# Score stacks of 64 rows in the two row halves of the TensorE array, and the steps of the first attention in pairs

## The reference

```python
# layer 0: keys are the context's 361 and the 100 own rows
qkv = _layernorm(x) @ w_attn + b_attn
q, k, v = jnp.split(qkv, 3, axis=2)
kc, vc = jnp.split(ctx @ w_ref + b_ref, 2, axis=2)
key, value = concat([kc, k]), concat([vc, v])
w = einsum('bhtd,bhsd->bhts', qh, kh) / sqrt(16)    # masks, and -2 on the context's columns
a = einsum('bhts,bhsd->bhtd', softmax(w), vh)
x = x + tanh(g_xattn[0]) * (a @ w_proj + b_proj)
x = x + tanh(g_ffn[0]) * quantised_ffn(_layernorm(x))          # 704 wide, rounded to 8 bits
# layer 1: queries from x, keys and values from the context alone
scores = einsum('bhqd,bhkd->bhqk', query, key) / sqrt(16)
x = x + tanh(g_xattn[1]) * (einsum('bhqk,bhkd->bhqd', softmax(scores), value) @ w_o.T + b_o)
x = x + tanh(g_ffn[1]) * top2_of_8_experts(_layernorm(x))      # 1024 wide
```

## Time and profile before

| | us |
|---|---|
| three runs, median (lowest, highest) | 663.76 (663.71, 664.19) |
| the profiled execution, its span | 664.1 |
| PE busy in it | 515.1 (78%) |
| PEld busy | 356.1 (54%) |
| DVE busy | 429.5 (65%) |
| ACT busy | 297.8 (45%) |
| POOL busy | 162.6 (24%) |
| mean granted TensorE clock | 0.861 of full |
| the eight rounds of the first attention | 24.7, 24.6, 25.7, 23.1, 23.0, 23.0, 24.1; the last 19.6 |
| the eight rounds of the second attention | 13.6, 18.5, 17.2, 13.3, 14.1, 13.4, 14.5; the last 11.2 |

### The profile page before, as it was taken

How to read it: one execution, slowest core, us unless ns; L and a number is a source line. 1 busy time by engine, 2 the same in 40 slices (tenths; PEclk the granted TensorE clock), 3 DMA queues, 4 the chain that set the end, 5 groups by cost and what they waited for, 6 DMA issues and landing times. The chain is left out here.

```text
span 664.1 us, 15475 instructions
## 1 busy us (share of the span) xinstructions
PE 515.1 (78%) x5403; PEld 356.1 (54%) x5403; DVE 429.5 (65%) x921; ACT 297.8 (45%) x482; POOL 162.6 (24%) x191
## 2 busy tenths in 40 slices
PE   2477798998988898737547878998975269999994
PEld 1263365665666667523223545655654258887782
DVE  7365576667686774387754856777569875666662
ACT  6442145556556538203314546676753223333331
POOL 5500022122122211010045410122125044444432
PEclk9989588979999977668659788999976569999997
DMA  9136834444535700000073787789347111222210
GB/s 258 40 120 113 161 82 105 105 115 110 112 99 140 188 5 25 1 1 0 0 154 88 181 155 151 142 165 178 121 158 270 60 40 28 48 40 47 49 19 1
DMA packets 73247, 64.31 MB, mean 97 GB/s; under 512 B 33326, under 2 KB 65750, under 8 KB 73190
## 3 DMA queue, kind: packets, MB, share of 16 engines
q1 hardware_dynamic: 61544, 41.37, 28.3%
q0 software_dynamic: 8224, 21.06, 12.0%
q10 hardware_dynamic: 3424, 1.12, 0.8%
HBM read 48.59 MB, written 15.92 MB: 97 GB/s over the span
## 5 line engine op out<-in xcount | busy, mean ns | idle before, releaser
L467 PEld LDWEIGHTS PS<-QS,KS 112*120 112x120 f16 (+2 forms) x896 | 81.9, 144 | 29.9 <-issue 10.9
L467 PE MATMUL PS<-QS,KS 112*120 112x100 f16 (+2 forms) x896 | 92.8, 229 | 5.1 <-ACT PT L530 3.7
L578 DVE CUSTOM_DVE_ANT_0 PS<-PS,maskv 100x461 f32<-100x461 f32 x128 | 80.5, 647 | 15.2 <-PE PS L436 14.3
L581 DVE TENSOR_REDUCE mx<-PS 100x1 f32<-100x361 f32 x128 | 63.6, 529 | 35.8 <-PE PS L439 34.7
L530 ACT ACTIVATE PT<-PS 120x400 f32<-120x400 f32 (+1 forms) x128 | 63.4, 503 | 45.5 <-PE PS L467 43.1
L530 ACT ACTIVATE PT<-PS,ctxb 120x400 f32<-120x400 f32 (+1 forms) x96 | 57.0, 596 | 52.7 <-PE PS L467 51.9
L436 PE MATMUL PS<-KS,QS 65*100 65x461 f16 x128 | 52.6, 416 | 17.9 <-DVE mx L578 17.3
L795 POOL TENSOR_SCALAR_AFFINE_SELECT PT<-PT 100x400 f32<-100x400 f32 x32 | 17.7, 553 | 187.6 <-ACT PT L530 187.6
L2025 PE MATMUL PS<-aT,WE 128*128 128x128 f16 x960 | 59.4, 224 | 0.0
L2025 PEld LDWEIGHTS PS<-aT,WE 128*128 x960 | 57.0, 101 | 0.0
L2038 PE MATMUL PS<-WE,hidden_high 128*128 x160 | 53.0, 379 | 0.0
(11 more groups left out here) (307 smaller groups left out, 1069.7 us busy)
## 6 DMA issues: line engine op xcount, KB each, us to landing
share<-in_L_ffn_w_dram POOLq DMA_DIRECT2D x13, 1024.0 KB, 9.3
k_scratch<-share SPq DMA_DIRECT2D x32, 180.5 KB, 2.5
KS<-k_scratch SPq DMA_DIRECT2D x32, 180.5 KB, 3.6
KS<-k_scratch SPq DMA_DIRECT2D x64, 90.2 KB, 6.3
QS<-q_scratch SPq DMA_DIRECT2D x64, 50.0 KB, 2.7
v_scratch<-xn SPq DMA_DIRECT2D x8, 385.7 KB
values_staged<-v_scratch SPq DMA_DIRECT2D x8, 385.7 KB
WE<-in_L_ffn_w_dram POOLq DMA_DIRECT2D x2, 1024.0 KB, 8.6
```

What stands on the lines that cost most here:

```text
L467: last = nc.tensor.matmul(bank[0:kn, i * T:(i + 1) * T], KS[p][:, h, k0:k0 + kn], QS[p][:, h, :], start=True, stop=True)
L578: nc.vector.tensor_tensor_reduce(rows, rows, maskv[:, :], 1.0, -BIG, ALU.add, ALU.max, mx[p][:, h:h + 1]).then_inc(s_smf, 1)
L581: nc.vector.tensor_reduce(mx[p][:, h:h + 1], sm_bank[h % 2][0:T, 0:TC], X, ALU.max).then_inc(s_smf, 1)
```

## The change

Of the four products of halves the one of the two low halves is left out of the scores. A head's stack now has 64 rows: 0 to 31 the query's high half against both key halves, 32 to 47 the delta and maximum rows, 48 to 63 the query's low half against the key's high half. The stacks of even batches lie at partitions 0 to 63, those of odd ones at 64 to 127, so that SM of batch o+1 and ST of batch o use different row halves of the array. SM reads all 64 rows; the rows of the maxima are zero at that time, which a third, zero plane of the queries' DRAM copy provides with each load. Per half of the heads a stack takes 7 loads (QS 3, own keys 2, context keys 2), of key bytes 3 parts instead of 4. In the second attention it is 3 for QS, and 2 for a group's keys, of 32 and 16 rows.

In setup ACT's two copies and the clearing of zero rows go; one POOL copy spreads `delta` over both key stacks at once (128 partitions x 7376), DVE clears QS (128 x 1600), two DMAs write the zero plane.

Steps of the first attention go in pairs: PE runs SM, ST, SM, ST of two steps, and then the T, K, V groups and the PV that the two steps had; ACT does both exponentials before the copies, DVE both maxima before the differences. In the second attention SM goes ahead of ST (a second SM behind it), and the unread matmul and PV follow.

```diff
-    KROWS = 4 * DH
-    IROW = 96
-    KX = IROW + H
+    KX = 4 * DH
+    IROW = 2 * DH
...
-        KSa = in_all("KS", [P, 2, H, S0], F16)
-        KS = [KSa[0:KX, p] for p in range(2)]
-        QS = [in_all(f"QS{p}", [KX, H, T], F16) for p in range(2)]
+        KSa = in_all("KS", [P, H, S0], F16)
+        QSa = in_all("QS", [P, H, T], F16)
+        KS, QS = ([a[p * KX:(p + 1) * KX] for p in range(2)] for a in (KSa, QSa))
...
         def pe_SM(pe, j, o, h, layer, smn):
-                nc.tensor.matmul(bank[0:T, 0:S0], QS[p][0:KROWS + 1, h, :], KS[p][0:KROWS + 1, h, :],
-                                 start=True, stop=True).then_inc(s_smd, 1)
...
+            n = S0 if layer == 0 else TC
+            nc.tensor.matmul(bank[0:T, 0:n], QS[p][:, h, :], KS[p][:, h, 0:n], start=True, stop=True
+                             ).then_inc(s_smd, 1)
...
         def act_max_rows(act, j, o, part, nmc):
-            nc.scalar.activation(QS[p][IROW:KX, hs, :], misc[NB][0:H, 0:T].unsqueeze(1).to_broadcast([H, n, T]),
+            nc.scalar.activation(QS[p][IROW:IROW + H, hs, :], misc[NB][0:H, 0:T].unsqueeze(1).to_broadcast([H, n, T]),
...
         def sp_queries_in(sp, j, o, mb):
-                sp.dma_start(QS[o % 2][s_:KROWS:2, hs, :], src).then_inc(s_ks[o % 2][mb], 16)
+                sp.dma_start(QS[o % 2][s_:IROW:2, hs, :], q_dram[hs, 0, :, ts].rearrange("h d t -> d h t")
+                             ).then_inc(s_ks[o % 2][mb], 16)
+            sp.dma_start(QS[o % 2][IROW:KX, hs, :], q_dram[hs, 1:3, :, ts].rearrange("h a d t -> (a d) h t")
+                         ).then_inc(s_ks[o % 2][mb], 16)
         def sp_keys_in(sp, j, o, hs, dst, dram, own, done):
-            for a in range(2):
-                sp.dma_start(dst[a * 2 * DH:(a + 1) * 2 * DH, hs, :], src).then_inc(done, 16)
+            sp.dma_start(dst[0:IROW, hs, :], src.rearrange("h d s t -> (d s) h t")).then_inc(done, 16)
+            sp.dma_start(dst[IROW + H:KX, hs, :], src[:, :, 0, :].rearrange("h d t -> d h t")).then_inc(done, 16)
...
@@ SP, setup
+                sp.wait_ge(s_kz, 1)
+                for mb in range(KC):
+                    sp.dma_start(q_dram[mb * HM:(mb + 1) * HM, 1, :, :],
+                                 QSa[:, 0:HM, :].rearrange("p h t -> p (h t)")).then_inc(s_qw, 16)
...
+                sp.wait_ge(s_kr, 1)
                 sp.wait_ge(s_kw[0][0], KW)
                 for mb in range(KC):
                     sp_stack0(sp, 0, 0, mb)
...
@@ POOL, setup
-                nc.gpsimd.memset(KS[0][KROWS:IROW, HM:H, :], 0.0)
-                nc.gpsimd.memset(KS[1][KROWS:IROW, 0:HM, :], 0.0)
-                nc.gpsimd.memset(KS[1][KROWS:IROW, HM:H, :], 0.0).then_inc(s_kz, 1)
+                nc.gpsimd.tensor_copy(KSa[:, :, :], delta[:, :].unsqueeze(2).to_broadcast([P, H, S0])).then_inc(s_kr, 1)
...
@@ ACT, setup
-                act.wait_ge(s_dl, 1)
-                for p in range(2):
-                    nc.scalar.activation(KS[p][IROW:KX, :, :], delta[:, :].unsqueeze(2).to_broadcast([H, H, S0]), ACT.Copy
-                                         ).then_inc(s_kr, 1)
                 act.wait_ge(s_wr[0], 16)
                 nc.scalar.activation(wah[:, :, :], r_attn, ACT.Copy, scale=WS).then_inc(s_wh8, 1)
...
@@ PE, rounds of the first attention
-                    for t in range(16):
-                        if t == 4:
-                            pe.wait_ge(s_vsb[u], j + 1)
-                        pe_ST(pe, j, u, t, 0, 0, 0)
-                        if t == NTURN0 and not first:
+                    for t in range(0, 16, 2):
+                        for i in (t, t + 1):
+                            if nxt:
+                                pe_SM(pe, j, u + 1, i, 0, 0)
+                            if i == 4:
+                                pe.wait_ge(s_vsb[u], j + 1)
+                            pe_ST(pe, j, u, i, 0, 0, 0)
+                        if t == NTURN0 - 1 and not first:
                             pe_turn(pe, j, u - 1, 0)
...
@@ PE, rounds of the second attention
                     for t in range(NST1):
+                        sms = SMH1[t] if nxt else 0
+                        if sms > 0:
+                            pe_SM(pe, j, o + 1, h, 1, SMN)
+                            h += 1
                         pe_ST(pe, j, o, t, 1, STN, 2 * B)
+                        if sms > 1:
+                            pe_SM(pe, j, o + 1, h, 1, SMN)
+                            h += 1
                         unread()
...
-                            for _ in range(SMH1[t]):
-                                pe_SM(pe, j, o + 1, h, 1, SMN)
-                                h += 1
```

More of the change, by code:

```diff
@@ L881, in round0 @@
                     nh0 = MISC0 + MISCR * (2 * j + u)
-                    for t in range(16):
-                        act_exp(act, j, u, t, 0, 0)
-                        if t == 0 and not first:
-                            act_max_rows(act, j, u, 1, 0)
-                        if t == 1 and not first:
-                            act_evac(act, j, u - 1, 0)
-                        if weights and 1 <= t < 1 + NIB + KC:
-                            rounding(NIB + t - 1)
-                        kind = TVK.get(t, "")
-                        if keys and kind[:1] == "T":
-                            act_hi_T(act, j, u + 2, int(kind[1]), nh0 + int(kind[1]))
-                        elif keys and kind[:1] == "K":
-                            act_hi_K(act, j, u + 2, int(kind[1]), nh0 + NK0[int(kind[1])])
+                    for t in range(0, 16, 2):
+                        for i in (t, t + 1):
+                            act_exp(act, j, u, i, 0, 0)
+                            if i == 0 and not first:
+                                act_max_rows(act, j, u, 1, 0)
+                        for i in (t, t + 1):
+                            if i == 1 and not first:
+                                act_evac(act, j, u - 1, 0)
+                            if weights and 1 <= i < 1 + NIB + KC:
+                                rounding(NIB + i - 1)
+                            kind = TVK.get(i, "")
+                            if keys and kind[:1] == "T":
+                                act_hi_T(act, j, u + 2, int(kind[1]), nh0 + int(kind[1]))
+                            elif keys and kind[:1] == "K":
+                                act_hi_K(act, j, u + 2, int(kind[1]), nh0 + NK0[int(kind[1])])
                     if nxt:
@@ L1013, in _ @@
             def _(dve):
-                for p in range(2):
-                    nc.vector.memset(QS[p][KROWS:IROW, :, :], 0.0)
-                nc.vector.memset(KS[0][KROWS:IROW, 0:HM, :], 0.0)
+                nc.vector.memset(QSa[:, :, :], 0.0).then_inc(s_kz, 1)
                 dve.wait_ge(s_x, 32)
@@ L1099, in round0 @@
                     nv = n0 + (NV0 if keys else 0)
-                    for t in range(16):
-                        if t == NTURN0 and not first:
-                            dve_norm(dve, j, u - 1, 0)
-                        if first and t == 8:
-                            dve_bias_in(dve, 0)
-                        if weights and t in WMT:
-                            weight_maxima(WMT.index(t))
-                        kind = TVK.get(t, "")
-                        if keys and kind[:1] == "T":
-                            dve_lo_T(dve, j, u + 2, int(kind[1]), n0 + int(kind[1]), nh0 + int(kind[1]))
-                        elif keys and kind[:1] == "K":
-                            k = int(kind[1])
-                            dve_lo_K(dve, j, u + 2, k, n0 + NK0[k], nh0 + 2 + k)
-                        elif nxt and kind[:1] == "V":
-                            dve_V(dve, j, u + 1, int(kind[1]), nv + int(kind[1]))
-                        if nxt:
-                            dve_max(dve, j, u + 1, t, 0, 0)
+                    for t in range(0, 16, 2):
+                        for i in (t, t + 1):
+                            if nxt:
+                                dve_max(dve, j, u + 1, i, 0, 0)
+                        for i in (t, t + 1):
+                            if i == NTURN0 and not first:
+                                dve_norm(dve, j, u - 1, 0)
+                            if first and i == 8:
+                                dve_bias_in(dve, 0)
+                            if weights and i in WMT:
+                                weight_maxima(WMT.index(i))
+                            kind = TVK.get(i, "")
+                            if keys and kind[:1] == "T":
+                                dve_lo_T(dve, j, u + 2, int(kind[1]), n0 + int(kind[1]), nh0 + int(kind[1]))
+                            elif keys and kind[:1] == "K":
+                                k = int(kind[1])
+                                dve_lo_K(dve, j, u + 2, k, n0 + NK0[k], nh0 + 2 + k)
+                            elif nxt and kind[:1] == "V":
+                                dve_V(dve, j, u + 1, int(kind[1]), nv + int(kind[1]))
                     if nxt:
@@ L1642, in _ @@
```

(2 more changed lines are left out.)

71 lines of the change are left out of this document (33 added, 38 removed).

## The result

The changed kernel takes 683.18 us (681.87 to 685.47) against 663.98 of the kernel before: 1.0279 times as long, 95% interval 1.0243 to 1.0315. The forecast was 658, in 646 to 670. The profiled execution has a span of 680.7 us for 664.1, and a mean granted clock of 0.813 for 0.861.

What follows compares the result with a forecast made beforehand. PE was taken to bound both attentions, ACT and DVE setup. From the profiled 664.1: -4.6 setup, -7.4 first attention, +4.0 clock, +2.4 second attention, -0.5 transfers = 658.0; median 657.7, forecast 658, range 646 to 670.

Steps and rivals of the forecast that it cites:

- Setup, -4.6: Setup: without ACT's two copies `wah` and `wal` start earlier, first projection at 20.3 for 24.93; 4.6 us less.
- the cover: Setup: POOL's one large copy of `delta`, from 16.65 to 43, beside DVE; at worst 1.8 of the gain goes.
- Steps of the first attention, -7.4: First attention: hidden SM -2.0, switches of tiling +0.65, pairs' waits +0.3; -1.05 a round, -7.4 us in seven rounds.
- Second attention, +2.4: Second attention: SM hidden saves up to 2.5, 20 more switches cost 2.6 to 3.0; +0.3 a round, eight rounds.
- Clock, +4: First attention: less PE work at round starts, waits left; one and a half more spells of 1.2 GHz, 4 us more.
- one and a half spells: First attention: added falls to 1.2 GHz charged, at 2.7 us each; 4 us, ends 0 and 8.
- My rival of the clock: First attention: the clock falls in every round, 10.8 us for 4.0, so 665 in all; chance 0.13.
- The slow rival, switches are dear: Unread matmul, second attention, and switches in the first: 0.21 each, 15.6 us more, 673 in all; chance 0.17.
- No two halves at once: Both attentions: matmuls of different halves run in turn, without drain; 661, 660.8 as a median; chance 0.11.
- Transfers, -0.5: Loads: fewer key bytes save 1.0 of second-attention query waits, a seventh load per stack half costs 0.5; -0.5 us.

Runs made afterwards that it cites:

- the first experiment: The changed kernel with POOL's copy of delta in two halves of the heads, one before its first reciprocal roots, one after x's first low half; 675.8 us.
- the edit of SM: The kernel before with SM reading rows 0 to 95 (64 to 95 zero) in place of 0 to 64; median 659.4 us against 666.0, ratio 0.9935.

## Why the prediction was wrong, and where it was right

**Setup, -4.6 forecast, +1.5 measured.** One step that failed is the cost of POOL's copy beside DVE. I took the 2.92 us of the earlier trace rows as a rate, 3.6 ns an element; most of it was a wait. The same trace has the same copy in 0.90 to 0.91 us five times of eight, as here (timeline),

```profile
396.49 0.90 POOL L1553 COPY xT<-values_staged 121x816 f32<-121x816 f32 x1 [11.28 <-DMA values_staged<-v_scratch]
```

and the three longer ones each begin during one long DVE instruction (L1512, 2.3 to 2.5 us). The copy of `delta` goes at 6.32 / 7376 = 0.86 ns. And I let DVE pay "half as much again", where it paid the copy's whole rest. The Trainium skill, "SBUF — State Buffer", "SBUF: two separate sides", has the rule: DVE and GpSimd share a pair of ports under an exclusive lock, held for a whole instruction, and the other one blocks; of DVE's instructions it names those in a mode with two ports and those with two inputs in SBUF, the latter only against a POOL instruction that reads SBUF. No trace shows the mode that `bcol` runs in, but the times agree: 0.57 became 6.85 beside 6.32, and where POOL only clears, in the kernel before, `wal` with its two inputs took 1.76 in the middle of this memset (timeline),

```profile
19.77 3.16 POOL L775 MEMSET KS<- 32x3688 f16 x1
```

and 1.75 in the first experiment with POOL idle. The reason I gave for the cover, that POOL cleared memory there before, was thus no reason: a copy isn't a memset. Nor does a copy hold every DVE instruction: in the 128-row kernel with the queries first, `ql` (L276) took 1.05 at 25.16, inside a copy of 6.33 from 22.96, and 1.05 outside of it. What the traces don't show is why `bcol` lost although it begins 0.50 ahead of the copy in the profile.

**Steps of the first attention, -7.4.** By the round the sum came out, its terms did not; the stage lost 0.4, since the clock took 7 to 12 us (below). Rounds with the same mean clock, 0.93, can be laid side by side (windows): the kernel before; 96 rows, in pairs; 64 rows in one half, in pairs and with passages; the changed kernel, which adds the sharing.

```profile
105.46:130.09 24.63, 22.12 (x265) 15.25 (x261) 16.20 (x46) 13.62 (x25) 4.52 (x9) 0.93 0.45 110
145.83:169.91 24.08, 22.39 (x263) 15.42 (x263) 15.91 (x46) 13.41 (x25) 4.52 (x9) 0.93 0.40 101
101.64:126.01 24.37, 23.05 (x262) 15.30 (x261) 16.09 (x46) 13.53 (x25) 4.51 (x9) 0.93 0.41 100
151.24:174.86 23.62, 21.20 (x263) 13.89 (x262) 15.85 (x46) 13.40 (x25) 4.51 (x9) 0.93 0.42 103
```

Over all such rounds pairs gain about 0.5 where I charged 0.3, passages cost 0.3 to 0.4 for 0.65, and the sharing saves 0.6 to 1.1 for 2.0. A step at full clock does save the 0.19 (0.23 for 0.42), but a round gets only part of it. In sum five rounds of 23.27 to 23.74 stand against 24.63: -0.9 to -1.4 for the forecast -1.05, right by luck, as errors of both signs cancelled; no round of the changed kernel was all at full clock, so the 22 expected there wasn't tested.

**Second attention, +2.4.** The sum has a slip: I hid SM in eight rounds, and the last has none, only its passages; 7 x 0.3 + 20 x 0.13 = 4.7 would have been its own figure. Of the +14.0 measured the clock took 16 to 26 (next paragraph), so the rest is between -2 and -12, 2.7 of it from shorter waits for queries (4.9 us for the 7.6 of the earlier trace rows). A passage cost about what was said; so either more was hidden by sharing than the 2.5 I took, or fewer passages lay on the path. No run tells which.

**Clock, +4.** This is the step that failed and turned the sign: what ran at 1.2 GHz. It rose by 57 - 34 = 23 us in the first attention and by 67 - 14 = 53 in the second. If PE bounds all of that time half of it is lost, 12 and 26 us (an estimate, and the upper end). Between the kernels with 65 and 96 rows, whose lists are the same, a us at 1.2 GHz cost 0.32 in the first attention and 0.30 in the second, where the waits for queries grew from 4.4 to 12.8 us as the clock rose; by that it is 7 and 16 us. So the clock took 23 to 38 us, not 4. I saw that busy share didn't tell rounds that lost the clock from those that kept it, and stopped there, with one and a half spells as if by chance. What I didn't ask is what else about PE's work the change alters, though it is in its title: the height. In the second attention I charged no clock at all. My rival of the clock was the right one, but it had the emptier round start as its cause, only for the first attention, and was priced at 665.

**The slow rival, switches are dear,** came nearest to the total (673) for the wrong reason: a passage costs 0.10 to 0.14, not 0.21, and taking most of them away left the second attention as long. *No two halves at once* is refuted by SM and ST starting at the same 184.25.

**Transfers, -0.5.** Small here: 2.7 us less of waits for queries in the second attention. But it goes with the slow rounds: at full height the new loads brought 12.8 to 14.1 us of waits there against 7.6 before, with 65 rows 4.4, and with 64 rows, all at 1.2 GHz, none. That the third load of a half is behind it, and not the new key loads, is likely but wasn't shown.

What stays open: by which measure rows enter, and why 65 lies so far from 96. That 128 rows are better than 96 in the second attention wasn't shown.

## What to carry to other kernels

A packed, half-height matmul saves time on the array and may cost the clock: before packing, look for spells of 1.2 GHz in the windows of before, and after it compare time at 1.2 GHz first. Where rows are free, more rows of zeros can be a cheap way to hold the clock: here the edit of SM was worth 0.65%. And price a POOL copy as time in which DVE may stand still, and look for an instruction whose length makes no sense for its size, as no wait showed it here.

## What the runs showed of the hardware that I had not expected

- With every stack matmul over the same 64 rows, PE was busy for 184.28 of 186.40 us in the second attention and stayed at 1.2 GHz all along; with 96 rows, 32 of them zeros, the same list had 0.92 of full clock. The Trainium skill, "TensorE: Matmul & The Clock Gate", "What's actually happening", has the clock set by how busy PE has been; with busy time as the profile counts it these runs don't agree, since the 96-row stage had PE busy for only 104.88 of 123.90 us.
- Two 64-row matmuls in different halves, with their weight loads, start within 0.03 us of each other and together take 0.23, for an SM of 0.20 and four ST of 0.22 alone. The passage between 64-row and 128-row matmuls takes 0.10 to 0.14.
- POOL's broadcast copy of f16 goes at 0.86 ns an element of a partition (6.32 for 7376) and one held a DVE instruction of 10 elements for 6.85 us, while another left DVE's `ql` at 1.05.
